# Stacking query and key parts: two hops through a buffer outside the chip, or sixteen direct transfers

## What is computed

```python
def _L1_gnn_ref(x, adj, Wq, bq, Wk, bk, Wv, bv, Wo, bo, gamma, beta):
    ...
    q = (x @ Wq + bq).reshape(b, n, H, HD)          # H = 8 heads of HD = 32
    k = (x @ Wk + bk).reshape(b, n, H, HD)
    ...
    scores = jnp.einsum('bnhd,bmhd->bhnm', q, k) * scale
    scores = jnp.where(mask, jnp.float32(-jnp.inf), scores)
    attn = jax.nn.softmax(scores, axis=-1)
```

## Time and profile before

| | |
|---|---|
| median of 3 runs | 1342.07 us (1337.53 to 1342.69) |
| profiled execution, its own time | 1347.88 us |
| its span, first to last instruction | 1346.2 us |
| PE, DVE, ACT, POOL busy | 90%, 78%, 65%, 36% of the span |
| mean granted PE clock | 0.965 |
| transfers of one iteration for the stack | 2 of 512 KB out, 16 of 128 KB back |

### The profile page before, as it was taken

One profiled execution on the slowest core, in us unless ns is written; L12 is line 12 of the kernel. 1 busy time (PEld: TensorE's weight loads), 2 busy tenths in 40 slices (PEclk: granted clock), 3 DMA queues, 4 the chain that ended last, 5 costly groups with the idle time before them and its releaser, 6 DMA issues.

```text
span 1346.2 us, 31660 instructions
## 1 busy us (share of the span) xinstructions
PE 1217.7 (90%) x9440; PEld 854.9 (64%) x9440; DVE 1051.1 (78%) x2769; ACT 879.7 (65%) x2018; POOL 487.3 (36%) x338
## 2 busy tenths in 40 slices
PE   5456999999999999999999999999999999999886
PEld 4234667766666766666676666667666666767464
DVE  2456778878797887879788787978878787987676
ACT  2224677767667677766767676677767676676574
POOL 1322144244253325325332532533352352334220
PEclk9778999999999999999999999999999999999899
DMA  6134135251624525162442516244252624423130
GB/s 187 32 78 122 52 77 159 56 146 47 156 63 94 140 66 136 47 160 58 97 137 69 133 47 162 56 100 134 70 132 62 156 62 109 109 70 102 49 79 32
DMA packets 177437, 129.38 MB, mean 96 GB/s; under 512 B 107904, under 2 KB 161152, under 8 KB 177408
## 3 DMA queue, kind: packets, MB, share of 16 engines
q1 hardware_dynamic: 175248, 121.15, 35.9%
q0 software_dynamic: 2160, 7.87, 1.5%
HBM read 61.87 MB, written 25.17 MB: 65 GB/s over the span
## 4 chain that ended last, share of the span: by engine, by line
PE 47%; DVE 24%; issue 11%; ACT 6%; DMA 6%; POOL 3%; SPq 2%; DVEq 1%; ACTq 0%; POOLq 0%
PE ps_j L642 18%; PE ps_t L655 10%; DVE masked_s L881 7%; PE ps_j L743 7%; PE ps_s L628 4%; PE ps_s L634 4%; ACT probs L793 4%; DVE y_l L1020 3%; DVE stats_L L901 2%; DVE y_l L978 2%; DMA xt<-ys 1%; SPq L456 1%; DMA bounce<-parts 1%; POOL ys L524 1%; DMA x<-x_dram 1%
## 5 line engine op out<-in xcount | busy, mean ns | idle before, releaser
L793 ACT ACTIVATE probs<-masked_s,nm_h 128x512 f32<-128x512 f32 x512 | 367.6, 718 | 153.0 <-DVE nm_h L881 148.3
L655 PE MATMUL ps_t<-ident,probs 128*128 128x128 f32 x2560 | 394.9, 277 | 24.5 <-ACT probs L793 23.9
L655 PEld LDWEIGHTS ps_t<-ident,probs 128*128 128x128 f32 x2560 | 303.3, 142 | 128.6 <-issue 53.7
L881 DVE CUSTOM_DVE_ANT_0 masked_s<-ps_s,mask_h 128x512 f32<-128x512 f32 x512 | 341.8, 683 | 35.1 <-issue 18.4
L799 ACT ACTIVATE pt_h<-ps_t 128x512 f32<-128x512 f32 x376 | 221.2, 588 | 110.6 <-PE ps_t L655 110.0
L634 PE MATMUL ps_s<-stack 128*128 128x512 f16 x512 | 196.3, 383 | 26.0 <-DVE nm_h L881 20.1
L642 PE MATMUL ps_j<-xw,pt_l 128*128 128x256 f16 x1536 | 188.1, 275 | 15.0 <-DVE qt L996 8.7
L509 POOL TENSOR_TENSOR rstd_L<-var_eps_L,minus_half 128x4 f32<-128x4 f32 x32 | 32.8, 1024 | 410.6 <-DVE var_eps_L L911 410.6
L642 PEld LDWEIGHTS ps_j<-xw,pt_l 128*128 128x128 f16 x1536 | 150.0, 99 | 47.7 <-DVE qt L996 12.8
L888 DVE COPY pt_h<-ps_t 128x512 f32<-128x512 f32 x136 | 93.6, 688 | 62.2 <-PE ps_t L655 61.9
L743 PE MATMUL ps_j<-pt_h,v 128*32 128x256 f32 x2048 | 141.6, 423 | 0.1
(11 more groups left out here) (96 smaller groups left out, 1727.5 us busy)
## 6 DMA issues: line engine op xcount, KB each, us to landing
stack<-bounce SPq DMA_DIRECT2D x256, 128.0 KB, 3.4
bounce<-parts SPq DMA_DIRECT2D x32, 512.0 KB, 3.4
adj_t<-adj_dram SPq DMA_DIRECT2D x31, 512.0 KB, 4.1
x<-x_dram SPq DMA_DIRECT2D x16, 512.0 KB, 4.3
mask_a<-mask_a SPq DMA_DIRECT2D x16, 512.0 KB, 2.9
mask_h<-mask_a SPq DMA_DIRECT2D x64, 128.0 KB, 2.4
out_dram<-y_f POOLq DMA_DIRECT2D x15, 512.0 KB, 5.4
pt_h<-l_wq SPq DMA_DIRECT2D x2, 256.0 KB, 4.4
```

What stands on the lines that cost most here:

```text
L655: last = pe.transpose(ps_t[r % 2][:, t], probs[:, r, t * P:(t + 1) * P], ident[:])
L793: act.activation(probs[:, r], masked_s[:, r], ACT.Exp, bias=nm[:, n, r:r + 1], scale=-1.0, accum_out=total[:, n, r:r + 1]).then_inc(exps, 1)
L881: dve.tensor_tensor_reduce(out=masked_s[:, r], in0=ps_s[r % 2][:], in1=m[:, r], scale=-scale, scalar=NONE_LEFT, op0=ALU.add, op1=ALU.min, ...
```

## The change

The write to `bounce` and the wait for it go away, and the buffer with them. stack_parts now waits for the parts and for the old stack's readers, and then issues sixteen transfers of 64 KB, from `parts` to `stack` directly, head by head: for head g and block s the 32 partitions of that head, with the query part and the key part that block s needs, go to the 32 partitions of block s in both planes at once. On the source side the two parts are 1 KB pieces apart from each other (side by side for s = 2), on the destination side they are 2 KB in one piece. PE's wait counts 16 transfers where it counted 8. ACT, before it writes new high parts, waited for the write to `bounce` of the graph before; it now waits for all sixteen transfers.

```diff
+STACK_PARTS = 16
...
-        bounce = nc.dram_tensor("bounce", [DC, 4, HD, 4, N], fp16).ap()
...
-        bounced = [sem(f"bounced{c}") for c in range(DC)]
...
-                sp.dma_start(bounce[c].rearrange("g d a n -> (g d) a n"), parts[:, c]).then_inc(bounced[c], 16)
-                sp.wait_ge(bounced[c], 16 * (b + 1))
-                settle(sp)
                 if not early(tiles, 1):
                     sp.wait_ge(scores_done, tiles)
                     settle(sp)
-                for s in range(4):
-                    qa, ka = s // 2, 2 + s % 2
-                    for dst, a in ((0, qa), (1, ka)):
-                        sp.dma_start(stack[HD * s:HD * s + HD, 4 * c:4 * c + 4, dst, :],
-                                     bounce[c, :, :, a, :].rearrange("g d n -> d g n")).then_inc(stacked[c], 16)
+                for g in range(4):
+                    for s in range(4):
+                        qa, ka = s // 2, 2 + s % 2
+                        sp.dma_start(stack[HD * s:HD * s + HD, 4 * c + g],
+                                     parts[HD * g:HD * g + HD, c, qa:ka + 1:ka - qa]).then_inc(stacked[c], 16)
...
-                        pe.wait_ge(stacked[n // 4], 16 * 8 * (b + 1))
+                        pe.wait_ge(stacked[n // 4], 16 * STACK_PARTS * (b + 1))
...
-                        act.wait_ge(bounced[l], 16 * b)
+                        act.wait_ge(stacked[l], 16 * STACK_PARTS * b)
```

## The result

| | before | changed |
|---|---|---|
| median | 1341.32 us (1337.53 to 1342.69, 4 runs) | 1374.87 us (1371.76 to 1379.34, 4 runs) |
| profiled execution, its span | 1346.2 us | 1373.8 us |
| mean granted PE clock | 0.965 | 0.963 |

A forecast was written before the change was run, and what follows sets the result against it. The prediction took PE's chain to bound the kernel, with the stack's transfers hidden nearly everywhere. Its parts, prologue +0.2, first iteration 0, loop +0.2 and tail +0.3, summed to +0.7 on 1342.07, so 1343 us; range 1335 to 1352.

The forecast's parts named there:

- Cost of the sixteen issues: SP's queue: 0.505 us per issue, 7.58 us to the last issue's start and 8.04 to its end.
- the prologue: Before the loop: the stack takes 10.18 us for 9.95, +0.2; ends 2.2 saved or 1.6 added.
- the first iteration: PE's 1.64 us wait for the stack goes, but DVE's idle time for mask rows stays: 0 (end −1.6).
- the loop: x's slightly later arrival counts only in the three iterations where PE waited for it: +0.2.
- the tail: After the loop: stack landed 10.18 us after the start, for 10.07 to PE's start: +0.3; ends −1.3 and +1.7.
- signs of being wrong: Issues of 0.55 us or more, growing landings, POOL idle over 1 us longer, PE mostly waiting for `xt<-xs`, other long-interval count.
- the cover of 1.5 us: In the loop, head 0's stack lands at 661.45 and is needed at 662.98, so it costs 0.
- Landing: The last stack transfer lands in 2.6 us, ends 1.9 and 4.0, with nothing queued up.
- Loop, x: x issued 8.70 us after stack_parts(1) begins, for 7.98, and used 4.05 after issue, for 4.71: together +0.06.
- The first rival: Each transfer costs more: at t = 0.64 some 17 us by x, prologue and tail 2.4 each, about 1365; chance 0.15.
- The second rival: Small transfers finish one behind another: sixteen take 30 us, 22 more than now, 300 us over 14 iterations; chance 0.02.
- The third rival: In the loop, earlier arrivals spare falls of PE's clock, 2.6 us each; half of nine give 1330; chance 0.09.

The follow-up runs named there:

- half_0: The kernel before with heads 0 to 3 by sixteen direct transfers, heads 4 to 7 still by the buffer: 1350.5 us, ratio 1.0086.
- half_1: The kernel before with heads 4 to 7 by sixteen direct transfers, heads 0 to 3 still by the buffer: 1371.17 us, ratio 1.0227.
- x_first: The changed kernel with stack_parts(1) put behind the next iteration's load of x and first load of adj: 1328.46 us, ratio to before 0.9914.
- by_head: The changed kernel with one semaphore per head, so PE waits only for the four transfers of the head it needs: 1366.68 us, ratio to before 1.0202.
- wide_eight: The changed kernel with eight transfers of 128 KB over 128 partitions in place of the sixteen, scores being other numbers: 1323.72 us, ratio to before 0.985.
- wide_sixteen: The changed kernel with its sixteen 64 KB transfers each over all 128 partitions, scores being other numbers: 1365.88 us, ratio to before 1.0199.
- bounce_x_first: The kernel before with stack_parts(1) put behind the next iteration's load of x and first load of adj: 1318.67 us, ratio 0.9853.

## Why the prediction was wrong

**The step that failed is the price of an issue**, in "Cost of the sixteen issues": "I take 0.465 + 0.04 = 0.505 us each, since the mask copies have the same kind of source and destination". Measured: 0.597 + 0.045 = 0.645. The mask copies were read correctly, but each of them was issued after a wait; none showed what a transfer within the chip costs right behind another. The eight reads did stand in a row, but their source was the other memory. I put a value of isolated issues into a burst of sixteen, and the sum's high end came from the landing, none from the issue. Part by part: the prologue, +0.2, was +5.05 (1.5 of it ahead of the stack); the first iteration, 0, was +4.56; the loop, +0.2, was +16.4; the tail, +0.3, was +1.6. Of the signs of being wrong that the prediction names, issues of 0.55 us or more and waits for `xt<-xs` in most iterations both came.

**Bottleneck and mechanism**: right in the main. The roads by which a longer queue would hurt, x behind stack_parts(1) and head 0 behind stack_parts(0), are the two that the trace shows, and half_0, half_1, x_first and by_head take them apart. That x counts far more than the stack was right too; head 0 came late in every iteration, against the cover of 1.5 us, but that cost time only outside the loop. What the prediction lacked is that x times POOL, and POOL, DVE: the loop had 25 us to win from an earlier x where I saw 1.7.

**Landing**: I took 2.6 us, it is 2.0; the queued-up transfers are gone, as forecast, and x is used 4.12 us after its issue for a forecast of 4.05 (Loop, x). The page of the Trainium skill ("SBUF — State Buffer", "Door 1: The DMA port swizzle") that gives 32 partitions half of the ports played no part, as forecast: one transfer of 66 kB in 0.645 us is 102 GB/s, far from the 231 of rows 8, and 128 partitions did no better. (Those 231 are 6% above the 218 GB/s that the page gives, so the agreement noted in the prediction is a rough one.)

**The first rival** had this very case: t = 0.64, a chance of 0.15, about 1365 us. In the loop it said 17 us and the trace shows 16.4, which is in part luck: by its sum x costs 1.2 us in nine iterations and 2.2 in three, where PE waited 35.3 us for it and won some back from DVE. What it lacked is the start: it gave the prologue and the tail 2.4 us each, and by the loop's second x the changed kernel is 9.6 us behind. Of that 1.5 lie before the first stack transfer; the stack of head 0 was waited for 4.25 us instead of 1.96, and in the first iteration stack_parts(1) took 12.13 us. "First iteration: 0" was wrong: both halves were late there. The range ended at 1352, short of a rival that no row had excluded.

**The second rival** fell: transfers overlap. The Trainium skill's 0.95 us for one of 64 KB ("DMA: Bandwidth & Descriptors", "Bandwidth"; for a load from HBM issued by GpSimd) is not how the sixteen add up; they go at 0.645. But the advice there to batch transfers, which I had weighed by transport alone, held here by another mechanism, the pace per transfer: wide_eight moves the same bytes in half the transfers and is 42 us faster than wide_sixteen.

**The third rival**, the clock, misread its rows: the short interval of rows 12 has a fall too (0.98), and one of the nine long ones has none. The 2.6 us that it took for the price of a fall are mostly DVE's conversion beside POOL; a fall with nothing in its way cost 0.7 to 1.0 us in bounce_x_first. The granted clock did fall less often, eight times for ten between the loop's second x and its last, but the loop was longer all the same.

## What to carry to other kernels

Price a burst by rows of a burst: the duration of an issue after a wait is its own work, the duration right behind another of its kind is the queue's pace, and the second can't be read from the first. Giving up a slow hop in favour of twice as many short ones is a trade in queue time; count what stands behind the last of them, and if that is a load with a small cushion, first try to put it ahead. A small sum of waits for some data doesn't say that having them earlier is worth nothing: look at what else stands behind them on the list of an engine that has time to spare, and what that runs into. Here it was POOL's work on x, the end of a layer norm behind it, and DVE's conversion.

## What the hardware showed that was not expected

DVE's conversion of 128x1024 values from int32 to bf16 took 0.68 us alone and 2.03 to 2.06 us when it began 0.9 us after an addition of POOL over 128x1024 fp32, ending 0.55 us behind it.

Transfers within the chip, issued by SP one behind another, went at one in 0.63 to 0.65 us whether they had 32 or 128 partitions, 64 or 128 KB, one piece or two; alone, the wide one-piece ones took 0.465 us to issue. Reads from outside the chip had no such pace (the old eight: 3.63 us together), but an issue whose source is in two pieces and whose destination is in one took 0.55 to 0.6 us instead of 0.41. What in the chip sets the pace is not known from these runs, nor whether a second queue would have one of its own; that was not tried.
